# Attention's first queries and keys evacuated by token range, the rest whole and spread by transfers, and a score lead that grows from 8 to 12

## What is computed

```python
q = layernorm(x) @ Wq.T + bq;  k = ctx @ Wk.T + bk;  v = ctx @ Wv.T + bv   # 32 query heads, 8 key groups, 8 wide
scores = q . k / sqrt(8), masked by a 128x128 mask and by a padding mask of each batch
x = x + tanh(g_xattn) * (softmax(scores) @ v @ Wo.T + bo)
# experts: the router's two best of 16 for each token, with renormalised weights
h_e = silu(y @ gate_e) * (y @ up_e)        # y = layernorm(x), 96 wide
x = x + tanh(g_ffn) * sum over e of combine_e * (h_e @ down_e)
```

## Time and profile before

| | |
|---|---|
| Time, median of 3 runs | 269.31 us (268.87 to 269.36) |
| Span of the profiled execution | 267.6 us |
| The profiled execution's own time | not given beside its span; the median is 1.7 us above the span |
| TensorE matmul busy | 237.8 us (89%) |
| VectorE busy | 188.0 us (70%) |
| ScalarE, POOL busy | 96.7 us (36%), 90.8 us (34%) |
| Mean granted TensorE clock | 0.959 of full |

### The profile page before, as it was taken

How to read it: one execution, slowest core, us unless ns; L and a number is a source line. 1 busy time by engine, 2 the same in 40 slices (tenths; PEclk the granted TensorE clock), 3 DMA queues, 4 the chain that set the end, 5 groups by cost and what they waited for, 6 DMA issues and landing times.

```text
span 267.6 us, 3780 instructions
## 1 busy us (share of the span) xinstructions
PE 237.8 (89%) x1275; PEld 168.9 (63%) x1275; DVE 188.0 (70%) x388; ACT 96.7 (36%) x173; POOL 90.8 (34%) x103
## 2 busy tenths in 40 slices
PE   0874889897789999999968999989999999999993
PEld 0751345454546555556544588768888888888883
DVE  2689786958877777675793377769767665766565
ACT  1575023857746565564546521111111010101000
POOL 6266008030081417361160110406936633562000
PEclk9997556999999999999999999999999999999998
DMA  7945400001100000211011000001322102000004
GB/s 208 159 129 127 109 1 2 0 0 43 39 0 1 2 0 7 55 21 37 1 26 35 1 2 0 0 0 39 82 61 60 38 21 61 0 0 2 0 0 158
DMA packets 20595, 10.25 MB, mean 38 GB/s; under 512 B 14400, under 2 KB 20064, under 8 KB 20576
## 3 DMA queue, kind: packets, MB, share of 16 engines
q1 hardware_dynamic: 20272, 9.79, 15.5%
q10 hardware_dynamic: 304, 0.22, 0.3%
HBM read 7.91 MB, written 1.05 MB: 33 GB/s over the span
## 4 chain that ended last, share of the span: by engine, by line
PE 74%; DVE 14%; ACT 5%; issue 3%; DMA 2%; ACTq 0%; DVEq 0%
PE bank L878 66%; ACT q L527 3%; PE bank L939 2%; DMA wkv_n<-in_L_xattn_Wv 2%; DVE q L629 2%; PE bank L918 2%; DVE mneg L740 2%; PE bank L935 1%; DVE xn L620 1%; DVE x_sb L871 1%; DVE w L782 1%; PE bank L952 1%; DVE xT L626 1%; PE bank L944 1%; DVE k L629 1%
## 5 line engine op out<-in xcount | busy, mean ns | idle before, releaser
L878 PE MATMUL bank<-xT,cT 128*128 128x512 f32 x288 | 70.2, 392 | 0.0
L878 PEld LDWEIGHTS bank<-xT,cT 128*128 128x128 f32 x288 | 53.7, 188 | 12.0 <-issue 0.8
L740 DVE TENSOR_REDUCE mneg<-bank 128x4 f32<-128x512 f32 x64 | 43.7, 687 | 19.6 <-PE bank L878 18.9
L585 ACT ACTIVATE pT<-bank 128x512 f32<-128x512 f32 x64 | 38.3, 601 | 28.4 <-PE bank L878 27.3
L572 ACT ACTIVATE pT<-bank 128x512 f32<-128x512 f32 x24 | 14.4, 598 | 84.2 <-PE bank L878 84.2
L878 PEld LDWEIGHTS bank<-w_d,q 128*128 128x128 f32 x288 | 37.1, 188 | 2.8 <-issue 1.3
L878 PE MATMUL bank<-q,kz 112*128 112x512 f32 x64 | 38.8, 609 | 0.0
L878 PE MATMUL bank<-w_d,q 128*128 128x256 f32 x288 | 38.0, 281 | 0.8 <-DVE q L818 0.8
L878 PE MATMUL bank<-kz,q 96*128 96x512 f32 x64 | 30.6, 484 | 5.9 <-DVE mneg L740 3.2
L411 POOL TENSOR_TENSOR vare<-mv,cst 128x1 f32<-128x1 f32 (+1 forms) x10 | 1.9, 194 | 82.4 <-DVE mv L614 80.4
L878 PE MATMUL bank<-cmask,ident_b 128*128 128x512 bf16 x64 | 28.4, 444 | 0.0
(11 more groups left out here) (119 smaller groups left out, 312.0 us busy)
## 6 DMA issues: line engine op xcount, KB each, us to landing
padf<-in_L_ffn_down_w SPq DMA_DIRECT2D x12, 128.0 KB, 2.3
c_sb<-in_ctx SPq DMA_DIRECT2D x2, 512.0 KB, 7.3
q<-q SPq DMA_DIRECT2D x8, 128.0 KB, 2.4
out<-x_sb SPq DMA_DIRECT2D x4, 256.0 KB, 2.4
c_sb<-in_L_ffn_gate_w SPq DMA_DIRECT2D x8, 96.0 KB, 2.2
c_sb<-in_L_ffn_up_w SPq DMA_DIRECT2D x8, 96.0 KB, 2.2
x_sb<-in_x SPq DMA_DIRECT2D x2, 256.0 KB, 3.6
x_sb<-in_x SPq DMA_DIRECT2D x1, 512.0 KB, 8.0
```

The lines of the kernel that those rows point to most:

```text
L585: nc.scalar.activation(pT[:, i // 4, i % 4, :], bank[2 + s % 2][:], ACT.Exp, scale=SCALE).then_inc(p_done, 1)
L740: nc.vector.tensor_reduce(mneg[:, r, 4 * hf:4 * hf + 4], bank[n % 2][:].rearrange("p (g k) -> p g k", g=4), X, ALU.max, negate=True).then_ ...
L878: return nc.tensor.matmul(dst, a, b, start=start, stop=stop, skip_group_check=True)
```

## The change

The first batch's 128 tokens (`NEAR`) of keys and queries are evacuated first, in the old form but 128 columns wide. The other 384 tokens of half 0 (`FAR`), and all of half 1, are evacuated whole, 128 partitions in one instruction, into `qc_hi` (which lies in xn for half 0 and in cT for half 1) and `qc_lo`; twelve DMAs of SP for each half then spread them over `q4`: for each of the high part, its copy and the low part, four. Score 8 and score 32, the first of batches 1 and 4, wait for all twelve. The far keys are evacuated behind the first eight scores. Two more bias columns hold the query biases in bank order, filled by four more small DMAs. The pad mask of batches 1 to 7 is converted by POOL instead of VectorE, and `cmask` of batch 0 is made alone, before batch 0's keys. Eight scores are done before slot 0; `RAMP` sets how many are issued by the end of slots 0 to 6, and from slot 7 on it is the old count. The x jobs of half 1 move to slots 6 and 7, its first q job to slot 9. The take of a q job is no longer split.

```diff
+RAMP = (8, 9, 11, 13, 15, 17, 19)
-        NBC = 2 * R + 3
+        NBC = 2 * R + 5
+        qc_lo = sb("qc_lo", [P, DC, TH], F32R)
+        qc_hi = [xn[:, 0:TPH]..., cT[0][:]...]
-        AT_SLOT = {("vn", 0): 0, ("wo",): 8, ("x", 1, 0): 5, ("x", 1, 1): 6,
-                   ("kv", 1): 3, ("q", 1, 0): 8, ("q", 1, 1): 11, ("vn", 1): 16}
+        AT_SLOT = {("vn", 0): 0, ("wo",): 8, ("x", 1, 0): 6, ("x", 1, 1): 7,
+                   ("kv", 1): 3, ("q", 1, 0): 9, ("q", 1, 1): 11, ("vn", 1): 16}
@@ issued
-            return min(CH, LEAD + s + 1)
+            if s < 0:
+                return G
+            return RAMP[s] if s < len(RAMP) else min(CH, LEAD + s + 1)
@@ sync
+            for c in range(DC):
+                for i in range(2):
+                    sp.dma_start(bperm[2 * R + 3 + c:2 * R + 4 + c, 2 * i * QR:2 * (i + 1) * QR].rearrange("a (h g d) -> a h g d", h=2, g=GH),
+                                 bq.rearrange("(a h g r d) -> a h g r d", a=1, h=2, g=GH, r=R)[:, :, :, 2 * c + i]).then_inc(d_b, 16)
+            def copy_near(r):
+                sp.wait_ge(near_hi, 2 + 2 * (r + 1))
+                sp.dma_start(q4[2 * QR:3 * QR, :, r, NEAR].bitcast(F32), q4[0:QR, :, r, NEAR].bitcast(F32)).then_inc(d_qn[r], 16)
+            def spread_queries(h):
+                at = FAR if h == 0 else slice(0, TH)
+                to = slice(h * TH + at.start, h * TH + at.stop)
+                if h == 0:
+                    sp.wait_ge(far_hi, 2 + DC)
+                else:
+                    sp.wait_ge(job_hi, hn["q", 1, DC - 1] + 1)
+                for k, qc in ((0, qc_hi[h]), (2, qc_hi[h]), (1, qc_lo[:])):
+                    if k == 1:
+                        sp.wait_ge(*emptied(("q", h, DC - 1)))
+                    for i in range(4):
+                        sp.dma_start(q4[k * QR:(k + 1) * QR, i % 2, i // 2::2, to].bitcast(F32),
+                                     qc[i * QR:(i + 1) * QR, :, at].bitcast(F32)).then_inc(d_qc[h], 16)
@@ gpsimd
-            pool.tensor_tensor(cmask[:], padf..., mqk..., ALU.add).then_inc(mask_ok, 1)
+            pool.tensor_tensor(cmask[:, 0], padf[:, 0:L], mqk[:], ALU.add).then_inc(mask_ok, 1)
             separate_keys(0)
+            step(pool.tensor_scalar(padf[:, L:NB * L], pad_u[:, L:NB * L], -BIG, None, ALU.mult))
+            pool.tensor_tensor(cmask[:, 1:NB], padf..., mqk..., ALU.add).then_inc(mask_ok, 1)
@@ scalar, before the context's second half
+                    keys_high(NEAR, near_hi)
+                    for c in range(DC):
+                        queries_near_high(c)
+                    sc.wait_ge(k_near, 2)
+                    keys_high(FAR, far_hi)
+                    take_values(0)
+                    for c in range(DC):
+                        sc.wait_ge(q_near, 2 * (c + 1))
+                        nc.scalar.activation(qc_hi[0][:, c, FAR], jbank(("q", 0, c))[:, FAR], ACT.Identity,
+                                             bias=bias[:, 2 * R + 3 + c:2 * R + 4 + c]).then_inc(far_hi, 1)
@@ vector
-            nc.vector.tensor_scalar(padf[:], pad_u[:], -BIG, None, ALU.mult).then_inc(masks_f, 1)
+            nc.vector.tensor_scalar(padf[:, 0:L], pad_u[:, 0:L], -BIG, None, ALU.mult).then_inc(masks_f, 1)
             take(("bias",))
-            take(("kv", 0))
-            take(("q", 0, 0))
+            keys_low(NEAR, near_hi, 0, k_near)
+            queries_near_low(0, (0, 1, 2, 3))
...
-            take(("q", 0, 1), (0, 1))
             for n in range(G):
                 row_max(n)
-                if n == 1:
-                    take(("q", 0, 1), (2, 3))
+                if n == 0:
+                    queries_near_low(1, (0, 1))
+                if n == 2:
+                    queries_near_low(1, (2, 3))
+                if n == 3:
+                    for c in range(DC):
+                        ve.wait_ge(far_hi, 2 + c + 1)
+                        queries_low(0, c, FAR)
             max_parts(0)
-            for n in range(G, LEAD):
-                row_max(n)
+            keys_low(FAR, far_hi, 0, k_ok)
             take(("c", 1, 0))
             take(("c", 1, 1))
@@ take, q of half 1 (ScalarE alike: one activation into qc_hi[1])
+                    ve.wait_ge(job_hi, hn[j] + 1)
+                    ve.wait_ge(d_qc[0], 16 * 3 * 4)
+                    queries_low(1, j[2], slice(0, TH))
@@ scores_q
+                if n == G:
+                    pe.wait_ge(mask_ok, 2)
+                if n in (G, TPH * G):
+                    pe.wait_ge(d_qc[b // TPH], 16 * 3 * 4)
...
-            for n in range(LEAD):
+            for n in range(G):
                 scores_q(n)
```

More of the change, by code:

```diff
@@ L205, in build @@
         brow_ok = sem("brow_ok")
[L207 removed]
+        d_qn = [sem(f"d_qn{r}") for r in range(R)]
+        d_qc = [sem(f"d_qc{h}") for h in range(NQ)]
+        near_hi = sem("near_hi")
+        far_hi = sem("far_hi")
+        k_near = sem("k_near")
+        q_near = sem("q_near")
         job_done = sem("job_done")
@@ L318, in takes_at @@
         def takes_at(s):
-            return ([(j, (2, 3)) for j in jobs_at(s - 2) if j[0] == "q"] +
-                    [(j, (0, 1) if j[0] == "q" else ALL) for j in jobs_at(s - 1)])
+            return jobs_at(s - 1)
         def toks(t):
@@ L500, in _, with high @@
             sc.dma_start(wkv_n[64:128, :], Wv).then_inc(d_wkv, 16)
-            def high(j, parts=ALL):
+            def high(j):
                 sc.wait_ge(job_done, jn[j] + 1)
@@ L524, in high @@
                 elif k == "q":
[L525 to L530, removed]
+                    ins = nc.scalar.activation(qc_hi[1][:, j[2]], ps[:], ACT.Identity,
+                                               bias=bias[:, 2 * R + 3 + j[2]:2 * R + 4 + j[2]])
                 elif k == "MT":
@@ L574, in _ @@
             for s in range(SLOTS):
-                for j, parts in takes_at(s):
+                for j in takes_at(s):
                     if j in hn or j[0] == "MT":
-                        high(j, parts)
+                        high(j)
                     if j == ("kv", 1):
@@ L629, in minus_biased, with keys_low, queries_near_low, queries_low @@
                 return nc.vector.scalar_tensor_tensor(dst, ps, col, hi.bitcast(F32), ALU.add, ALU.subtract)
-            def take(j, parts=ALL):
+            def keys_low(at, hi, n, done):
+                for hf in range(2):
+                    ve.wait_ge(hi, n + hf + 1)
+                    nc.vector.tensor_copy(k4[QR:2 * QR, hf, at], k4[0:QR, hf, at].bitcast(F32))
+                    minus_biased(k4[2 * QR:3 * QR, hf, at], jbank(("kv", 0))[QR * hf:QR * (hf + 1), at],
+                                 bias[0:QR, 2 * R + hf:2 * R + hf + 1], k4[0:QR, hf, at]).then_inc(done, 1)
+            def queries_near_low(c, parts):
+                for i in parts:
+                    ve.wait_ge(near_hi, 2 + 4 * c + i + 1)
+                    hf, r, src = i % 2, 2 * c + i // 2, QR * i
+                    ins = minus_biased(q4[QR:2 * QR, hf, r, NEAR], jbank(("q", 0, c))[src:src + QR, NEAR],
+                                       bias[0:QR, hf * R + r:hf * R + r + 1], q4[0:QR, hf, r, NEAR])
+                    if hf:
+                        ins.then_inc(q_near, 1)
+            def queries_low(h, c, at):
+                minus_biased(qc_lo[:, c, at], jbank(("q", h, c))[:, at], bias[:, 2 * R + 3 + c:2 * R + 4 + c],
+                             qc_hi[h][:, c, at]).then_inc(q_lo, 1)
+            def take(j):
                 ps, k = jbank(j), j[0]
@@ L843, in _ @@
                     elif j[0] != "MT":
-                        take(j, parts)
+                        take(j)
                 for n in ahead(s):
```

70 lines of the change are left out of this document (37 added, 33 removed).

## The result

The changed kernel takes 266.84 us (median of 4 runs, 266.45 to 267.21) beside 269.09 (268.52 to 269.36) for the kernel before in the same session: a ratio of 0.9911, interval 0.9893 to 0.9930. By the ratio it is faster by 2.4 us (2.3 by the medians); 4.6 were forecast. The profiled execution took 266.45 us with a span of 264.6, so some 1.8 us lie around the span; the prediction took 1.7.

What follows compares the result with a forecast made beforehand. The beginning was taken as bound by VectorE and ScalarE, TensorE waiting or at half clock. Gains of 2.2 us by slot 8 and 2.4 behind it made 4.6: span 267.6 to 263.0, time 264.7 us, range 262.0 to 268.5.

Steps and rivals of the forecast that it cites:

- Start and first scores: Opening up to VectorE's statistics: start 0.3 us later, first score at 19.1 instead of 21.07, statistics ending 6.1 us earlier.
- the slope: Evacuation price per column from 512 against 256 columns: ScalarE 0.89 ns, VectorE 1.04 ns; used for 128 and 384 columns.
- The added wait: Score 8 waits for twelve spreading DMAs, landing at 33.3 us; hidden behind VectorE's statistics until 33.4, so no cost.
- The new collision: VectorE reaches normalising the second half at 36.2, stands beside GpSimd's xb_sb until 40.1, and finishes at 41.2 instead of 47.21.
- The sum to slot 8: Normalising 6.0 us sooner, less 2.8 for maxima, 0.7 for transposing and 0.3 at the start: slot 8 2.2 us sooner.
- The clock in this sum: TensorE falls to half clock after score 7, about 30, and returns near 38, inside VectorE's block until 41.2: no cost.
- own last sign of being wrong: TensorE's clock: the prediction called itself wrong if half clock reappeared behind 41 us.
- Slower than before: Rival, 0.10: TensorE meets VectorE's block and 2.4 us of keys without stock; clock falls about 41, stays down: about 273.
- Second half: Second half's query evacuation behind slot 8: of 2.92 us of TensorE gaps 0.5 stay, gaining 2.4 us.
- Fall in the second gap: Rival, 0.22: clock holds at 28, falls while TensorE idles before maximum 11, to 41.9; recovery loses 3 us: 267.7.
- my own case: The whole sum coming true, centred on 264.7 us: chance 0.43, 263.2 to 266.2 us.
- VectorE first: Rival, 0.12: VectorE reaches normalising before 35.5, ahead of xb_sb, and ends at 36.9 instead of 41.2: 262.2 us.

Runs made afterwards that it cites:

- experiment 3: Changed kernel plus 27 unread matmuls filling TensorE's gaps between score 2 and slot 0: 267.38 us, ratio 0.9900 to the kernel before.
- experiment 6: Kernel before with only the second half's queries evacuated whole and spread by twelve DMAs: 266.90 us, ratio 0.9909 to the kernel before.
- experiment 1: Changed kernel with GpSimd's bo_b and xb_sb operations moved behind the keys of batch 3: 264.08 us, ratio 0.9791 to the kernel before.
- experiment 7: Kernel of experiment 6 with GpSimd's bo_b and xb_sb moved behind the keys of batch 3: 262.67 us, ratio 0.9730 to the kernel before.
- experiment 8: Kernel before with only GpSimd's bo_b and xb_sb moved behind the keys of batch 3: 264.49 us, ratio 0.9824 to the kernel before.
- Experiment 2: Changed kernel plus seventeen unread matmuls in TensorE's gaps of slots 4 and 5: 265.74 us, ratio 0.9850 to the kernel before.
- experiment 5: Changed kernel with half 1's queries again in 32-partition parts with four DMA copies: 271.89 us, ratio 1.0074 to the kernel before.
- experiment 4: Changed kernel plus both sets of unread matmuls, from Experiment 2 and experiment 3: 264.81 us, ratio 0.9827 to the kernel before.
- experiment 11: Changed kernel with bo_b and xb_sb moved, later keys' evacuation behind slot 5's maxima, and 27 unread matmuls before slot 0: 260.87 us, ratio 0.9678 to before.

## Why the prediction was half right

- **Start and first scores: right but for one price.** The first mask instruction ran 0.69 us later than before, at 14.52, the four small DMAs having taken 2.80 us (3.89 to 6.69) and not 1.44; that price was wrong and stayed hidden, since the first score waited for its query copy. First score 18.73 for 19.1: the 32 KB copy landed in 1.9 us, not 2.4. The small operations cost what the slope said, by the groups of ScalarE and VectorE between 14 and 75 us:
```profile
L583 ACT ACTIVATE q<-bank,bias 32x128 fp32r<-32x128 f32 x8 | 2.9, 360 | 0.2
...
L606 ACT ACTIVATE xn<-bank,bias 128x384 fp32r<-128x384 f32 x2 | 1.2, 582 | 1.7 <-DVE q L680 1.7
...
L680 DVE SCALAR_TENSOR_TENSOR q<-bank,bias,q 32x128 fp32r<-32x128 f32 x8 | 2.8, 346 | 0.2
```
0.36 and 0.35 us for 128 columns (0.34, 0.35), 0.58 for 384 on ScalarE (0.57). Statistics ended at 33.45 for 33.4.
- **The added wait: right in time, with less cover than thought.** Landed near 33.0 for 33.3, and hidden, but by TensorE's own half clock: where fillers hold the clock (experiment 3) TensorE waits 0.66 us for it.
- **The new collision: right in place and length, wrong in what followed.** `xb_sb` from 35.62 to 40.19 (35.5 to 40.1) and normalising ended at 41.32 (41.2). This agrees with "SBUF — State Buffer" of the Trainium skill, Who interferes with whom: VectorE came second, at 37.29 behind 35.62, and stood until GpSimd was done. In experiment 6, where VectorE's record begins 0.02 us ahead and VectorE stood as well, the records do not show who came first. I took that block as a fixed part of the schedule and priced only its end; experiments 1, 7 and 8 show 3.2 to 4.8 us that could be had by moving one operation.
- **The sum to slot 8: wrong, 0.14 us instead of 2.2.** The failed step is "The clock in this sum". It said that the clock falls once, between 28 and 38, in VectorE's cover. It fell at 25.9, came back at 36.2, right ahead of the two waits, and fell again at 42.9, where TensorE was soon the bound: the prediction's own last sign of being wrong, half clock behind 41. Experiment 2 prices that at 1.6 us and experiment 3 shows the first fall to be free. The 1.31 us wait that fed the fall is the second omission: the evacuation of the later keys, 2.4 us on VectorE, stood in the "Slower than before" rival as something TensorE would meet without scores in stock, and in the sum as nothing. Moved away, it is worth 2.3 us where the move has been made.
- **Second half: too low, 3.6 us instead of 2.4.** Of 2.92 us of gaps I kept 0.5. None is left. The other 0.7 us is TensorE's own busy time for the same 118 matmul records (21.26 us before, from 54.47 to 78.66, and 20.56 now, from 54.33 to 74.89); why it shrank is not shown. Experiments 5 and 6 give this part 4.4 and 2.5 us, by the ratio.
- **Rivals.** "Fall in the second gap" had the place right with 0.22, and its premise (a clock held at 28) wrong. The time, 266.8, lies between it and the upper end of my own case, 266.2, so the sum's own case missed and only the wide range held. That the miss is no larger is partly luck, since errors offset each other: the sum had 2.1 us too much at slot 8 and nothing for the 0.8 us lost behind the last addition, and 1.2 us too little in the second half. "VectorE first" did not happen: VectorE reached the normalising at 37.29, 1.7 us behind `xb_sb`. The outcome of "Slower than before" came only in experiment 5, with the old queries of half 1, and by 2 us instead of 4: waits at VectorE's block, a fall near 44, a return near 50, and a further fall at the second half's queries, not one fall that lasts.

Two forecasts in the experiments failed in the same manner: the price of the collision (experiments 7 and 8) was read from one execution's 2.61 us.

## What to carry to other kernels

Look for a long GpSimd operation that nothing needs soon and that runs beside VectorE's critical work, and move it before anything is rebuilt: here that alone gave twice the gain of the large change. An earlier start is worth only what the next shared bound lets through; follow it to the first point at which the old and the new schedule meet, and count there each wait that a drained stock of work exposes, with the fall of TensorE's clock that a wait can bring. Where the clock falls and returns in a kernel, give the forecast a term for it with both its ends, since one profile shows only one draw of it.

## What the runs showed of the hardware

**The moment at which the clock returns isn't set by the program alone.** The kernel before and that of experiment 8 are the same up to GpSimd's work near 40 us, and TensorE's records between 24.5 and 30.9 agree. The stretches, first of before, then of experiment 8:
```profile
24.50:30.90 6.40, 5.49 (x11) 2.31 (x11) 4.93 (x9) 0.00 (x0) 0.00 (x0) 0.50 0.66 144
31.50:36.00 4.50, 4.50 (x11) 2.20 (x11) 3.31 (x8) 0.00 (x0) 0.00 (x0) 0.50 0.01 3
```
```profile
24.50:30.90 6.40, 5.49 (x11) 2.31 (x11) 4.93 (x9) 0.00 (x0) 0.00 (x0) 0.50 0.67 148
31.50:36.00 4.50, 3.23 (x13) 1.54 (x12) 4.08 (x9) 0.65 (x2) 0.00 (x0) 1.00 0.01 2
```
With 5.49 us busy in 6.40 in both, the kernel before comes back to 2.4 GHz at 44.2 us and that of experiment 8 near 31. The fall differed too: near 23.7 us before and at 21.0 in experiment 8, although the first score starts at 21.07 in both. Runs of one kernel that differ in time differ in clock as well (experiment 7: 261.38 us at a mean clock of 0.980, 264.76 at 0.961), and the 0.4 us of experiment 4, where it hardly falls (0.995 to 1.000), agree with that. It is not the only reason: the runs of experiment 11 stand at 0.994 to 1.000 too and spread over 1.4 us.

**It fell and returned where the earlier trace rows had not led me to expect it.** It fell behind a stretch of 5.70 us with 3.33 us of matmuls, much fuller than the 1.22 in 5.40 of before, and in that stretch no gap was longer than 0.91 us. It returned after 5.4 and 4.0 us without a gap, where before it had taken 6.3.

**Small strided transfers cost SP more than large ones.** Four DMAs of 0.2 KB took 0.70 us each to issue (2.80 in all), against 0.64 for a spread of 96 KB.
